# Seven block products per pair of F chunks in the down projection of a four-layer residual kernel

## The reference

```python
B, N, H, F = (4, 64, 512, 1376)
gate = lora_add(jnp.einsum('bnh,fh->bnf', x, W_gate), x, A_gate, B_gate)
up = lora_add(jnp.einsum('bnh,fh->bnf', x, W_up), x, A_up, B_up)
act = jax.nn.silu(gate) * up
down = lora_add(jnp.einsum('bnf,hf->bnh', act, W_down), act, A_down, B_down)
return down
...
x = x + _L3_cond_ref(x, ...)
```

## Time and profile before

| | us |
|---|---|
| runs | 298.31, 298.38, 298.52 (median 298.38) |
| profiled execution | 298.5 |
| its span | 296.7 |
| PE busy | 286.5 (97% of the span) |
| DVE busy | 197.0 (66%) |
| ACT busy | 143.8 (48%) |
| POOL busy | 45.3 (15%) |

### The profile page before, as it was taken

How to read it: one execution, slowest core, us unless ns; L and a number is a source line. 1 busy time by engine, 2 the same in 40 slices (tenths; PEclk the granted TensorE clock), 3 DMA queues, 4 the chain that set the end, 5 groups by cost and what they waited for, 6 DMA issues and landing times.

```text
span 296.7 us, 4572 instructions
## 1 busy us (share of the span) xinstructions
PE 286.5 (97%) x1624; PEld 235.8 (79%) x1624; DVE 197.0 (66%) x343; ACT 143.8 (48%) x255; POOL 45.3 (15%) x67
## 2 busy tenths in 40 slices
PE   5889999999999999999999999999999999999995
PEld 5358778888888788887788888888889888888884
DVE  1288897894656999897776776785747958342003
ACT  2378672513326279756646656566535783211000
POOL 1000000000804405243123213403000000000000
PEclk9999999999999999999999999999999999999999
DMA  5999974008504040300440520600193100022005
GB/s 165 342 393 395 343 243 108 0 0 248 178 0 101 0 145 0 121 23 0 124 159 4 167 115 16 197 3 26 48 354 126 56 0 0 0 73 71 0 2 141
DMA packets 23255, 33.29 MB, mean 112 GB/s; under 512 B 2624, under 2 KB 15424, under 8 KB 23104
## 3 DMA queue, kind: packets, MB, share of 16 engines
q1 hardware_dynamic: 22944, 32.47, 33.0%
q10 hardware_dynamic: 288, 0.52, 0.6%
HBM read 30.89 MB, written 2.10 MB: 111 GB/s over the span
## 4 chain that ended last, share of the span: by engine, by line
PE 86%; DVE 5%; DMA 4%; issue 2%; ACT 1%; SPq 1%; DVEq 0%; ACTq 0%
PE bank L1237 12%; PE bank L1238 12%; PE bank L1239 12%; PE bank L1360 10%; PE bank L1361 10%; PE bank L1362 10%; DMA w_raw<-in_w 4%; PE bank L1342 3%; PE bank L1192 2%; PE bank L1485 2%; PE bank L1221 1%; PE bank L1284 1%; PE bank L1174 1%; PE bank L1222 1%; PE bank L1223 1%
## 5 line engine op out<-in xcount | busy, mean ns | idle before, releaser
L546 ACT ACTIVATE part<-bank 128x512 f32<-128x512 f32 x44 | 26.1, 594 | 30.3 <-PE bank L1362 30.2
L1237 PE MATMUL bank<-act_hl,wd_hl 128*128 128x512 f32 (+1 forms) x99 | 36.5, 369 | 0.0
L1238 PE MATMUL bank<-act_hl,wd_hl 128*128 128x512 f32 (+1 forms) x99 | 36.3, 367 | 0.0
L1239 PE MATMUL bank<-act_hl,wd_hl 128*128 128x512 f32 (+1 forms) x99 | 36.2, 366 | 0.0
L1052 DVE TENSOR_TENSOR part<-bank,part 128x512 f32<-128x512 f32 x44 | 29.1, 682 | 6.7 <-PE bank L1342 6.6
L977 DVE SCALAR_TENSOR_TENSOR bgu_st<-bgu_st,lo_rows,bgu_raw 128x512 fp32r<-128x512 f32 x22 | 17.6, 836 | 11.6 <-ACT bgu_st L546 11.6
L803 DVE TENSOR_TENSOR w_hl<-w_raw,w_hl 128x512 fp32r<-128x512 f32 x29 | 19.0, 688 | 9.1 <-ACT w_hl L546 9.1
L546 ACT ACTIVATE act_hl<-act_f 128x512 fp32r<-128x512 f32 x22 | 13.6, 624 | 20.8 <-PE bank L1239 18.8
L803 DVE TENSOR_TENSOR act_hl<-act_f,act_hl 128x512 fp32r<-128x512 f32 x22 | 14.9, 691 | 12.9 <-ACT act_hl L546 12.8
L546 ACT ACTIVATE w_hl<-w_raw 128x512 fp32r<-128x512 f32 x29 | 17.7, 624 | 8.9 <-DMA w_raw<-in_w 8.6
L1239 PEld LDWEIGHTS bank<-act_hl,wd_hl 128*128 128x128 f32 x99 | 18.6, 188 | 3.1
(11 more groups left out here) (162 smaller groups left out, 695.1 us busy)
## 6 DMA issues: line engine op xcount, KB each, us to landing
w_raw<-in_w SPq DMA_DIRECT2D x22, 256.0 KB, 7.2
wgu_raw<-in_wgu SPq DMA_DIRECT2D x11, 512.0 KB, 4.1
bgu_raw<-in_bgu SPq DMA_DIRECT2D x40, 128.0 KB, 2.7
w_raw<-in_w SPq DMA_DIRECT2D x7, 512.0 KB, 7.6
wd_raw<-in_wd SPq DMA_DIRECT2D x4, 704.0 KB, 6.0
out<-x_f SPq DMA_DIRECT2D x7, 256.0 KB, 2.3
x_f<-in_xT SPq DMA_DIRECT2D x6, 256.0 KB, 8.4
w_raw<-in_w SPq DMA_DIRECT2D x1, 1024.0 KB, 4.9
```

The source lines that it names most:

```text
L546: return act.activation(dst, src, ACT.Copy)
L1237: pe.matmul(dst, w_hi, x[0][:, cols], start=start, stop=False)
L1238: pe.matmul(dst, w_hi, x[1][:, cols], start=False, stop=False)
L1239: return pe.matmul(dst, w_lo, x[0][:, cols], start=False, stop=stop)
```

## The change

Ten of the chunks of F (1 to 10) become five pairs. For each pair the contraction over two chunks, times two pairs of output chunks and two halves of tokens, is a 2 x 2 block product, made of seven products instead of eight by the scheme that gate and up use already. The seven run one after the other, each over all five pairs (`down_product(k, banks, start)`: 5 pairs x 2 output chunks x 3 = 30 matmuls into two banks). The odd chunk 0 is a plain product (`odd_chunk`, 24 matmuls in all). What it adds:

- sums of tokens, four on DVE (`form_down_t`, 128x2560 each, within `act_f`)
- sums of weights, four on POOL (`down_sum`, five additions of 128x256 each, within `wd_raw`)
- splits of whole products' operands: 128x2560 of tokens and 128x1280 of weights per product, instead of 22 + 11 of 128x512
- copies of partial sums out of the banks on ACT (`copy_sum`, eight of 128x512), which POOL adds to `x_f` in 16 additions of 128x256 (`x_add_pre`); `x3_add` on DVE stays, eight times 128x512, and waits for them
- no output piece is cut in halves any more

Two splits are placed into step 10: `tokens_high(0)` after copy 0 and `weights_high(0)` after copy 1. The load of `wd_raw` keeps its place and its waits in SP's queue.

The core of the diff:

```diff
@@ gpsimd @@
+            def down_sum(k, dst, a, b, op):
+                if k > 0:
+                    pool.wait_ge(ds_formed, PAIRS * k)
+                for p in range(PAIRS):
+                    pool.tensor_tensor(dst[:, :, p], a[:, :, p], b[:, :, p], op).then_inc(ds_formed, 1)
...
+            for o in range(C):
+                pool.wait_ge(wd_in[o], 16)
+            pool.wait_ge(wc_lo, 3 * STEPS)
+            down_sum(0, s1_f, a21, a22, ALU.add)
+            down_sum(1, a21, a11, a21, ALU.subtract)
+            pool.wait_ge(dw_lo, 1)
+            down_sum(2, a11, s1_f, a11, ALU.subtract)
+            pool.wait_ge(dw_lo, 2)
+            down_sum(3, a12, a12, a11, ALU.subtract)
+            for n in range(len(PRE_ORDER)):
+                x_add_pre(n)
@@ scalar @@
                 copy_part(n, 0)
+                if not more:
+                    tokens_high(0)
                 copy_part(n, 1)
                 if more:
                     wc_high(n + 1, 1)
+                else:
+                    weights_high(0)
                 copy_part(n, 2)
@@ vector @@
+            weights_low(0)
+            tokens_low(1)
+            weights_low(1)
+            odd_act_low(0)
+            odd_wd_low()
+            form_down_t(0)
+            form_down_t(1)
+            weights_low(2)
+            tokens_low(2)
+            for h in range(H):
+                td_low(h)
+            form_down_t(2)
             dve.wait_ge(bd_hi, 1)
             low_rows(bd_st[:], bd_raw[:]).then_inc(bd_ready, 1)
...
+            tokens_low(3)
+            weights_low(3)
+            form_down_t(3)
+            tokens_low(4)
+            weights_low(4)
+            for i in range(2):
+                x3_add(i)
+            tokens_low(5)
+            weights_low(5)
+            tokens_low(6)
+            weights_low(6)
+            odd_act_low(1)
+            for i in range(2, len(DOWN_PIECES)):
+                x3_add(i)
@@ tensor @@
+            down_product(0, 6, True)
+            pe.wait_ge(td_sel_step, 1 + HB)
+            pe.wait_ge(c_added, 4 * STEPS)
+            for h in range(H):
+                spread_ranks(h)
+            down_product(1, 0, True)
+            pe.wait_ge(d0_lo, 2)
+            for i in range(2):
+                odd_chunk(i, False)
+            for i in range(2, C):
+                odd_chunk(i, True)
+            pe.wait_ge(td_lo, 4)
+            down_product(2, 2, True)
+            pe.wait_ge(bd_ready, 1)
+            for i in range(2):
+                down_lora(i)
+            pe.wait_ge(sum_copied, 2)
+            down_product(3, 6, False)
+            pe.wait_ge(sum_copied, 4)
+            down_product(4, 2, False)
+            pe.wait_ge(sum_copied, 6)
+            down_product(5, 6, False)
+            down_product(6, 4, False)
+            for i in range(2, C):
+                down_lora(i)
+            pe.wait_ge(d0_lo, 3)
+            for i in range(C, C + 2):
+                odd_chunk(i, False)
+                down_lora(i)
+            pe.wait_ge(sum_copied, 8)
+            for i in range(C + 2, 2 * C):
+                odd_chunk(i, False)
+                down_lora(i)
```

More of the change, by code:

```diff
@@ L55 @@
 W0_RING = 3
-ACT_RING = 8
 PAIRS = FC // 2
@@ L298, in td_block @@
             dst = td_st[rows, h * HT:(h + 1) * HT].rearrange("p (q b s) -> p q b s", b=2, s=S)
-            src = bank[6 + h][rows, 0:2 * S].rearrange("p (q s) -> p q s", s=S)
+            src = bank[2 + h][rows, 0:2 * S].rearrange("p (q s) -> p q s", s=S)
             return dst[:, :, par], src
-        DOWN_PIECES = [(o, slice(h * HT, (h + 1) * HT)) for h in range(H) for o in range(C)][:-1]
-        DOWN_PIECES += [(C - 1, slice(first, first + 2 * S)) for first in (T - 4 * S, T - 2 * S)]
-        def down_bank(o, cols):
-            last = o == C - 1 and cols.start == T - 2 * S
-            return bank[0 if last else (o if cols.start < HT else 4 + o)][:, cols.start % HT:(cols.stop - 1) % HT + 1]
+        DOWN_PIECES = [(o, slice(h * HT, (h + 1) * HT)) for h in range(H) for o in range(C)]
@@ new lines, in weights_of @@
+        def weights_of(k):
+            a = {(d, i): (pair_wd(wd_raw, d, i), pair_wd(wd_lo, d, i)) for d in range(2) for i in range(2)}
+            return ((a[0, 0][0], a11_hi[:], a11_lo[:]),
+                    (a[0, 1][0], a12_hl[:, 0], a12_hl[:, 1]),
+                    (s1_f[:], s1_hi[:], s1_lo[:]),
+                    (a[0, 0][0], s2_hi[:], a[0, 0][1]),
+                    (a[0, 1][0], s4_hi[:], a[0, 1][1]),
+                    (a[1, 0][0], s3_hi[:], a[1, 0][1]),
+                    (a[1, 1][0], a22_hi[:], a[1, 1][1]))[k]
@@ L1078, in zero_td_bank, with odd_act_low, odd_wd_low @@
+            def odd_act_low(h):
+                dve.wait_ge(td_tm, H)
+                dve.wait_ge(d0_hi, 1 + 2 * h)
+                low(act_lo[:, 0, h * HT:(h + 1) * HT], act_f[:, 0, h * HT:(h + 1) * HT], odd_hi[h][:]).then_inc(d0_lo, 1)
+            def odd_wd_low():
+                dve.wait_ge(d0_hi, 2)
+                low(wd_lo[:, :, 0], wd_raw[:, :, 0], wd0_hi[:]).then_inc(d0_lo, 1)
             def zero_td_bank(h):
@@ L1513, in spread_ranks @@
                 for q in range(2):
-                    ins = pe.matmul(bank[6 + h][:, q * S:(q + 1) * S], td_sel[:, q], td_sb[:, h], start=True,
+                    ins = pe.matmul(bank[2 + h][:, q * S:(q + 1) * S], td_sel[:, q], td_sb[:, h], start=True,
                                     stop=True)
```

296 lines of the change are left out of this document (200 added, 96 removed).

## The result

The changed kernel takes 307.19 us (median of four runs, 306.28 to 308.46) against 298.45 us of the kernel before: a ratio of 1.0277 (95% interval 1.0247 to 1.0307), 8.7 us slower. The forecast was 304.0, its range 299.8 to 307.5. So the direction was right and the time is inside the range, by 0.3 us, but it lies 3.2 us above the forecast, beside the 306.5 to 307 that were given to rival C.

The account below looks back on a forecast made before the run. TensorE was taken to bound the kernel before, VectorE to become the down projection's bound: 7.2 us saved, 13.1 in waits, 0.3 at the tail, less 0.5 of counting, giving a 304.0 median, range 299.8 to 307.5.

Parts of the forecast that it names:

- rival C: TensorE's 4 us standstills make the clock fall, the first costing 2.9 us more: 306.5 to 307 us; chance 15%.
- TensorE saves 7.2 us: Down projection: 234 products of 512 columns instead of 264, and no halves, save 7.2 us.
- the 0.5 of counting: The down projection before took 63.5 us, its own matmuls counted this way 63.0; 0.5 us taken off the sum.
- First wait, 4.6 us: Last gate and up step: ScalarE's weights' split awaits wd_raw's landing, making the seventh product 4.6 us late.
- VectorE's chain: Down projection: VectorE's work ahead of product five takes 34.5 us, plus 7.4 us lost to GpSimd.
- my list of meetings: VectorE instructions slowed by GpSimd ahead of products three, four, five: 7, 4 and 3, each losing 0.53 us.
- The waits ahead of products three, four, five: Down projection: TensorE waits for VectorE 2.8, 3.9 and 1.8 us.
- The tail: End of the kernel: the last addition is 512 wide instead of 256, costing 0.27 us more.
- The sum: Whole kernel: matmuls end at 298.4 instead of 292.95, span 302.4 us, with 1.8 around it 304.2, against the median 304.0.
- a granted clock under 1.0: Sign of being wrong, pointing to rival C; the forecast itself counted matmuls at a clock of 1.0.
- the sum with 0.74: Skill's exclusive-lock reading: each meeting costs VectorE 0.74 us, 10.4 in all, putting the sum 3 us higher; not used.
- rival A: Down projection: GpSimd's additions do not slow VectorE, the end comes 7.5 us earlier, 296.5 us; chance 10%.

Follow-up runs that it names:

- e4: Changed kernel with GpSimd's weights' sums and x_f additions cut (work left out) and the first weights' high part behind the last silu: 294.79 us, ratio 0.9848.
- e9: Kernel before with ScalarE's added wait for wd_raw and 14 idle matmuls ahead of the last step's seventh product: 302.63 us, ratio 1.0115.
- e3: Changed kernel with GpSimd's x_f additions and weights' sums cut to 2 of 128 columns or a zero fill (work left out): 300.48 us, ratio 1.0045.
- e0: Changed kernel again, without any edit, for a second profile: 307.54 us, ratio 1.0281.
- e6: Changed kernel with idle matmuls in TensorE's standstills, 14 ahead of the last step's seventh product, ten ahead of the third down product: 305.52 us, ratio 1.0214.
- e2: Changed kernel with GpSimd's 16 additions to x_f cut to 2 of every 128 tokens (work left out): 303.66 us, ratio 1.0152.
- e7: Changed kernel with two of the four pieces of wd_raw loaded earlier: 304.44 us, ratio 1.0187.
- e8: Changed kernel with GpSimd's 16 additions of 256 elements to x_f made as eight of 512: 308.28 us, ratio 1.0296.
- e10: Changed kernel with two pieces of wd_raw loaded earlier and the first weights' high part behind the last silu: 303.08 us, ratio 1.0119.
- e5: Kernel before with one addition, ScalarE waiting for all wd_raw pieces ahead of its third copy in the last step: 304.60 us, ratio 1.0198.
- e12: Changed kernel with early wd_raw loads, late first weights' split, later x_f additions and idle matmuls, all work done: 306.23 us, ratio 1.0241.
- e1: Changed kernel with the first weights' high part moved behind the last silu of the last gate and up step: 304.92 us, ratio 1.0206.

## Why the prediction was right, and where it was short

- **TensorE saves 7.2 us.** Confirmed: 6.7 after the 0.5 of counting, by e4.
- **First wait, 4.6 us.** The mechanism is as described: the third copy at 225.95, predicted 225.2; the seventh product at 226.59, predicted 225.85. Of these 0.74 us, 0.65 were there at the start of step 10 (214.52 against 213.87 of before). In the other profiles, of both kernels' variants, that start lies between 213.67 and 215.19, so this is scatter and not the change. Less it, the seventh product is 226.59 - 221.88 = 4.7 us late. e9 agrees: 3.7 us for the wait, and the 1.2 us of the weights' split, which e9 has not ahead of the copy, come on top.
- **VectorE's chain.** 41.9 us predicted (34.5 + 7.4), 42.0 measured (34.9 + 7.1, by e3), with 7, 4 and 3 slowed instructions ahead of products three, four and five, as counted. It begins at 233.18, predicted 231.85: 0.74 by the seventh product, 0.5 because an odd product at 230.69 met GpSimd (1.18 us instead of 0.69), which I had not counted since my list of meetings began only at the chain's start.
- **The waits ahead of products three, four, five.** Predicted 2.8, 3.9, 1.8; in the first profile 2.8, 2.3, 1.3, in e0 2.3, 3.9 and none. Their sum is smaller where the clock is low ahead of them: TensorE then spends the same time in slow matmuls instead of waiting. The starts are what counts: 255.43, 266.86 and 275.36, predicted 254.0, 265.2 and 273.8, each 1.4 to 1.7 late, by the chain's start.
- **The tail.** The last addition takes 0.69 us instead of 0.42, as said. From the end of the matmuls to the end of the span are 4.4 us, predicted 4.0; the stores' median landing time is 3.0 us against 2.4 in the earlier trace rows.
- **The sum.** For the profiled execution 306.28 against 304.2: 1.3 at the chain's start, 0.2 at product five, 0.2 behind it, 0.4 at the tail. That execution has no low clock behind the first wait; the median is 0.9 us above it. So of the 3.2 us between forecast and median the clock has between 0.9 and 2.0 (e6 against e0), and the rest is the list here. The range held the median by 0.3 us only, and it reached that far only because it took in rival C.
- **The step that failed is the clock.** The forecast took it as 1.0 and gave its fall 15%, and named a granted clock under 1.0 as a sign of being wrong; all eight executions of the changed kernel, the four of the result and the four of e0, show one (0.978 to 0.993). What the profiles show behind each of TensorE's waits of over 2 us in the stretch (clock by windows of 4 us):

| wait, us (profile) | granted clock behind it, lowest window |
|---|---|
| 2.2 to 2.4 (after, e0, e2, e7, e8, e10) | 1.0 |
| 2.8 (after), 3.0 (e7) | 0.63, 0.69 |
| 3.5 (after) | 1.0 |
| 3.4, 3.8, 3.6, 3.6, 3.4 (e5, e0, e2, e3, e8) | 0.50 to 0.71 |
| 3.8 (e10), 3.9 (e0), 3.9 (e6), 3.9 (e12), 4.6 (e8), 5.2 (e1) | 0.50 to 0.72 |

Of the fourteen waits of 2.8 us and more one passed without a fall, and none of the six of 2.2 to 2.4 us had one. The mechanism of rival C was right and should have been the likeliest case. Its price, 2.9 us, was too high for the median, 2.0 to 2.1 us (e5 and e9, e6 and e0): in e5's profile the clock is back at 1.0 from 228 us on and the loss is 1.55. In e0 all twelve products behind the wait are slow and TensorE loses 2.7, nearly the 2.9, of which 2.0 reach VectorE's chain. So not all of it is inherited, as C had it. The low clock behind a later wait costs nothing where the next product waits for VectorE anyway, as said in C for product four: in the first profile nine matmuls of product three are slow, 1.8 us, and product four still waits 2.26 us. It does cost where the fall comes behind the fourth product's wait: 1.05 us in e6 and 2.6 in e12.

The Trainium skill ("TensorE: Matmul & The Clock Gate", Part 1) has an idle TensorE drop from 2.4 to 1.2 GHz, and the runs here agree (0.427 us between matmuls in e0 behind a 3.77 us wait); I had given the rule too small a chance because no row of before held a standstill of that length. The Trainium skill ("SBUF — State Buffer", Who interferes with whom) calls the pair of ports that VectorE and GpSimd share an exclusive lock, which by the prediction's reading blocks the one engine for the other's whole instruction. Here the loss is 0.53 us for an instruction of 0.70 us alone and 1.1 for one of 1.28 alone (e8), so it grows with the instruction but stays some 0.2 us under it; the measurement decides, and the sum with 0.74 would have stood nearly 3 us higher, at about 307. That is nearer to the median than my 304.0, but by luck: the chain would then have taken 44.9 us, and it took 42.0.

One slip of the prediction changes nothing: in rival A the fourth product would itself wait 0.85 us (its operands are ready at 259.35, TensorE is there at 258.5), so TensorE reaches the fifth at 266.15 and not at 265.3, still ahead of the 266.3 that decides.

What stays open: whether the first wait can be removed without VectorE then meeting or waiting for GpSimd's sums. A version with GpSimd's sums on another engine was not tried. Why the stores land 0.6 us later is not settled either.

## What to carry to other kernels

A product scheme that saves matmuls pays in sums and splits of other engines, and these must fit into the time of the *shorter* TensorE phase, with 0.5 us added for each VectorE instruction with both inputs in SBUF that meets a GpSimd instruction of 256 elements per partition. Price a new wait of some 3.5 us on TensorE at its length plus some 2 us of low clock behind it, unless another wait follows that takes it in. Taking such a wait away need not return its price: see what else hangs on the same event (here GpSimd's sums: 2.7 us returned with them, 5.7 without). And do not fill a standstill with idle matmuls before looking whether it is still there.
